# Moving two groups of transposes ahead of the attention products in a fused conditional transformer block

## The reference, cut to what matters

```python
out = (input - mean) * jax.lax.rsqrt(var + EPS) * weight + bias     # layer norm, then + tanh(cond @ lin_w.T + lin_b)
_rmsnorm = lambda x: x * jax.lax.rsqrt(jnp.mean(x * x, axis=-1, keepdims=True) + EPS)
attn = jax.nn.softmax(scale * jnp.einsum('bnqd,bnkd->bnqk', q, k), axis=-1)
o = jnp.einsum('bnqk,bnkd->bnqd', attn, v)                           # then @ W_o.T
ffn = jax.nn.silu(x @ gate_w.T) * (x @ hidden_w.T) @ out_w.T + out_b
x = x + a_alpha * attention(gamma * _rmsnorm(x) + beta)
return x + f_alpha * ffn(gamma2 * _rmsnorm(x) + beta2)
```

## Time and profile before

| | us |
|---|---|
| median of 3 executions (995.45 to 999.46) | 995.79 |
| profiled execution, its own time | 997.22 |
| span of the profiled execution | 995.4 |
| TensorE matmul busy | 944.1 (95%) |
| TensorE weight loads busy | 906.4 (91%) |
| VectorE, ScalarE, GpSimd busy | 715.6, 615.2, 584.6 |

### The profile page before, as it was taken

The page is one execution under the profiler, slowest core; times in us unless marked ns, Lnnn a source line. Parts: engine busy times, 40 slices in busy tenths (PEclk is TensorE's granted clock), DMA queues, the critical chain, the costliest instruction groups (busy, mean ns, idle before and its releaser), DMA issues.

```text
span 995.4 us, 28347 instructions
## 1 busy us (share of the span) xinstructions
PE 944.1 (95%) x11164; PEld 906.4 (91%) x11164; DVE 715.6 (72%) x1355; ACT 615.2 (62%) x1733; POOL 584.6 (59%) x531
## 2 busy tenths in 40 slices
PE   5557899999999999999999999999999999999998
PEld 4446799999999999999999999999999999999997
DVE  6654687777777778777777777777777876766654
ACT  4343676667666766676667666766776676666432
POOL 4445765756667675757576575666757475544320
PEclk9776799999999999999999999999999999999999
DMA  7000001000010000001000100100010000000000
GB/s 234 22 23 1 23 2 33 13 12 33 13 33 4 31 13 18 27 13 34 13 23 13 34 13 12 34 12 33 2 33 13 12 13 13 13 12 12 12 12 22
DMA packets 20930, 23.33 MB, mean 23 GB/s; under 512 B 1216, under 2 KB 20288, under 8 KB 20800
## 3 DMA queue, kind: packets, MB, share of 16 engines
q1 hardware_dynamic: 20800, 21.54, 6.6%
HBM read 13.15 MB, written 8.39 MB: 22 GB/s over the span
## 4 chain that ended last, share of the span: by engine, by line
PE 92%; DVE 4%; issue 2%; POOL 1%; ACT 1%; DMA 0%; SPq 0%; DVEq 0%; ACTq 0%; POOLq 0%
PE psum L293 18%; PE psum L295 18%; PE psum L294 18%; PE psum L432 6%; PE psum L507 6%; PE psum L506 6%; PE psum L505 6%; PE psum L408 4%; PE psum L448 4%; PE psum L323 2%; PE psum L342 2%; DVE least L632 1%; PE psum L331 1%; PE psum L501 1%; PE psum L335 1%
## 5 line engine op out<-in xcount | busy, mean ns | idle before, releaser
L293 PE MATMUL psum<-xf_hi,ffn_hi 128*128 128x256 f32 x1024 | 289.6, 283 | 2.1 <-ACT probsT L908 1.6
L295 PE MATMUL psum<-xf_hi,ffn_lo 128*128 128x256 f32 x1024 | 286.0, 279 | 0.0
L294 PE MATMUL psum<-xf_lo,ffn_hi 128*128 128x256 f32 x1024 | 285.9, 279 | 0.0
L900 ACT ACTIVATE probs<-psum,least 128x64 f32<-128x64 f32 x928 | 204.6, 354 | 55.6 <-DVE least L632 55.0
L1096 POOL TENSOR_TENSOR probs<-probs,inv_sum 128x512 f32<-128x512 f32 x128 | 133.4, 1044 | 126.9 <-DVE inv_sum L653 126.2
L293 PEld LDWEIGHTS psum<-xf_hi,ffn_hi 128*128 128x128 f32 x1024 | 192.2, 188 | 3.2 <-issue 2.8
L295 PEld LDWEIGHTS psum<-xf_hi,ffn_lo 128*128 128x128 f32 x1024 | 192.4, 188 | 0.0
L294 PEld LDWEIGHTS psum<-xf_lo,ffn_hi 128*128 128x128 f32 x1024 | 192.0, 187 | 0.0
L929 ACT ACTIVATE prod_hi<-late 128x512 fp32r<-128x512 f32 x128 | 83.5, 653 | 114.3 <-DVE late L711 114.2
L507 PE MATMUL psum<-prod_hi,ffn_lo 128*128 128x256 f32 x512 | 143.2, 280 | 0.0
L506 PE MATMUL psum<-prod_lo,ffn_hi 128*128 128x256 f32 x512 | 143.0, 279 | 0.0
(11 more groups left out here) (106 smaller groups left out, 2244.6 us busy)
## 6 DMA issues: line engine op xcount, KB each, us to landing
out_t_dram<-x_res SPq DMA_DIRECT2D x31, 256.0 KB, 2.2
xin<-x_dram SPq DMA_DIRECT2D x15, 512.0 KB, 4.0
w_raw<-attn_w_dram SPq DMA_DIRECT2D x1, 1024.0 KB, 7.5
x_res<-gate_w_dram SPq DMA_DIRECT2D x1, 1024.0 KB, 10.2
late<-hidden_w_dram SPq DMA_DIRECT2D x1, 1024.0 KB, 11.7
w_raw<-out_w_dram SPq DMA_DIRECT2D x1, 1024.0 KB, 6.4
xin<-x_dram SPq DMA_DIRECT2D x2, 256.0 KB, 2.9
k_heads<-mod_w_dram SPq DMA_DIRECT2D x1, 320.0 KB, 4.4
```

Of the source, the lines that this page charges most:

```text
L293: pe.matmul(out, stat_hi, mov_hi, start=first, stop=False)
L294: pe.matmul(out, stat_hi, mov_lo, start=False, stop=False)
L295: return pe.matmul(out, stat_lo, mov_hi, start=False, stop=last)
L900: op = act.activation(probs[g % 2][:, h * SEQ:(h + 1) * SEQ], scores[g % 2][:, h // 2, h % 2], ACT.Exp, bias=least[g % 2][:, h:h + 1], sca ...
```

## The change

The two groups of norm transposes, with the waits for their bank, become a function `norm_item`. From slot 12 on it is called directly behind `turn_probs`, ahead of `score_banks_free`, `times_values` and `score`. Up to slot 11 it stays behind the scores. No instruction is added or taken away, and the other engines' lists are as they were.

```diff
+            def norm_item(s):
+                grp, j = s // PSEQ, s % PSEQ
+                norm_bank_free(s)
+                if j == 0 and is_part(grp + 2):
+                    turn_x(grp + 2)
+                if j == 2 and is_group(grp) and s >= 0:
+                    spread_inverses(grp)
+
@@
                     for g in (s - 2, s - 1):
                         if is_seq(g):
                             turn_probs(g)
+                    if s >= FFN_AT:
+                        norm_item(s)
                     score_banks_free(s)
@@
-                if s % 2 == 0 or s < 0:
-                    norm_bank_free(s)
-                if j == 0 and is_part(grp + 2):
-                    turn_x(grp + 2)
-                if j == 2 and is_group(grp) and s >= 0:
-                    spread_inverses(grp)
+                if (s % 2 == 0 or s < 0) and s < FFN_AT:
+                    norm_item(s)
```

## The result

The changed kernel has a median of 1004.93 us (1003.18 to 1005.39, 6 executions) against 998.08 for the kernel before, measured beside it (6 executions, one of them disturbed; 996.70 without that one); the ratio is 1.0067 with a 95% interval of 1.0052 to 1.0082, so slower by 6.7 us. 1000.0 us, a ratio of 1.0042, had been forecast with a range up to 1002.8. The disturbed execution, of 1838.4 us, is left out of the ratio.

A forecast was written before the change was run, and what follows sets the result against it. TensorE, busy without a gap from 140 to 900 us, was taken to bound the kernel. Full slots' +3.7 us and odd slots' +0.5 made +4.2 on 995.79, so 1000.0 us, with a range of 995.6 to 1002.8.

The forecast's parts named there:

- What bounds the kernel, and what the move does to TensorE's packing: TensorE has no gap from 140 to 900 us; four transposes cost 0.44 us in the new place, 0.37 in the old.
- Rival A: The gap behind the scores goes, the projection following at its usual step: -0.14 us a slot, 989 us; chance 0.08.
- rival B: Transposes cost 0.09 us each in the new place too, so full slots give 0: 996 us; chance 0.15.
- Its bounds: Transpose step in the new place: 0.09 us gives nothing, 0.12 gives 5.8 us; range stated as 999.0 to 1000.9 us.
- Its size: Full slots from first turned probability to first gate matmul: +0.07 us each, 53 of them, +3.7 us.
- The odd slots: Slots 12, 122, 126 and 130: +0.1, +0.07 at worst, +0.22 and +0.10 us, nothing in 134; together +0.5 us.
- The moved waits: Norm transposes ask 1.2 us earlier for bank, x or inverse RMS and still find them; margin 1.3 us.
- The scores come later: Scores 0.44 us later; ahead of hidden in inverse-RMS slots some 0.07 us of slack is left, wait costed at nothing.
- Rival C: New wait ahead of hidden in 27 inverse-RMS slots; 0.1 us beyond the slack adds 2.7 us, 1002.7 us; chance 0.22.
- The base: Median of the kernel before, 995.79 us, to which the forecast added 4.2 us.
- What would show it: Timeline signs: 4.16 us from first turned probability to gate, keys 0.67 us behind scores' start, no TensorE wait 140 to 900 us.

The follow-up runs named there:

- x_only: Changed kernel with only the transposes of x moved, those of the inverse RMS left behind the scores; 1.0016 of the kernel before.
- keep_even_inv: Changed kernel, but the inverse-RMS transposes of the even groups stay behind the scores; 1.0012 of the kernel before.
- before_late: Kernel before plus a 0.42 us VectorE instruction behind both least-score searches in even groups' inverse-RMS slots, spare tile placed behind `stats`; 1.0109 of the kernel before.
- late_even: Kernel before plus a 0.42 us VectorE instruction behind both least-score searches in even groups' inverse-RMS slots, spare tile behind all others; 1.0004 of the kernel before.

## Where the prediction was right and where it was wrong

- **What bounds the kernel, and what the move does to TensorE's packing**: right. The twelve transposes stand at steps of 0.11 us: 8 take 0.88 (510.35 - 509.47) and the four of x 0.53 with the gap behind them. The gap behind the scores moved ahead of the projection, as slot 120 had shown. Rival A, a gain, is refuted, and rival B, no change, too: a slot costs more.
- **Its bounds**: the prediction's own bounds of the step, 0.09 and 0.12 us, give 996.3 and 1002.1 us, not the 999.0 to 1000.9 that it gives its 0.55 for, and rival B stands at 996 in one place and at 995.6 in another.
- **Its size**: 0.05 instead of 0.07 us a slot. The term that was off is the distance from scores to keys, 0.62 us and not slot 120's 0.67; against that the first keys matmul holds the second back by 0.23 instead of 0.20. 2.7 us in place of 3.7 (2.5 unrounded). By the rule on tile shapes of TensorEngine Tiling (Array Packing) in the Trainium skill, Key Properties, the move would be free, since there are as many changes of shape as before; the trace has the gaps at these changes, alike in both kernels (0.20, 0.15 and 0.20 us from start to start, with 0.11 between transposes), but 0.05 us more a slot.
- **The odd slots**: in slot 126 +0.23 us came (0.22 forecast), in slot 130 +0.05 (0.10, with bounds 0 and 0.2). At the end of the stretch behind slot 124 nothing of it is left (85.33 and 85.34 us), which the prediction did not foresee: from 66 to 73 us behind slot 124, just behind a wait of both kernels, 60 matmuls of 256 columns stand 0.113 us apart in the changed kernel and 0.118 in the one before. Why they do is open. In slot 12 the transposes themselves cost the 0.1 us forecast, and the waits behind them, 0.8 us, had been left out.
- **The moved waits**: right. TensorE finds bank, x and inverse RMS ready; nothing is held up ahead of the transposes from 125 to 900 us.
- **The scores come later**: this is the step that failed. I followed the 0.44 us as far as hidden of the same slot, found 0.07 us of cover left, and costed the wait at nothing. That cover did hold: there is no wait ahead of hidden in the inverse-RMS slots. But "slots with the inverse RMS are where that counts" was wrong. VectorE is not the only one who waits for the scores: by way of the least scores ScalarE's exponentials do, and ScalarE, and VectorE behind it, hand the delay on without idle time of their own to take it up. It was still whole, 0.43 us, 14 us later in the next slot with x, where in odd groups the merge leaves no room and the squares' load stood 0.07 us behind its release. Price: 12 times 0.38 us, which is 4.6 us; with the like in slot 17 and in the group of slot 12 it is 5.6 us.
- **Rival C** had the mechanism, a wait of TensorE ahead of hidden from later scores, and the right sign, but the wrong slot, and 27 places where there were 12; the larger of the two waits, ahead of the squares, it did not have. Its condition ("from 0.07 us on") was that of a place where nothing happened. What spoke against it, that TensorE had no gap from 140 to 900 us before, was no argument: a list without waits doesn't tell how near they are. That the range's upper edge, 1002.8, was set from this rival, and lies near what the ratio makes of 995.79 (1002.5), is luck.
- **The base**: 1004.93 us is 4.9 us above the forecast, but the change is only 2.5 us dearer than forecast by the ratio (6.7 for 4.2). The rest is the 995.79 on which the forecast stood, a median of three; beside the experiments the kernel before has medians of 997.23 to 997.53, from 14 to 29 executions.
- **"What would show it"** served: 4.14 us a slot (4.16 forecast), but a wait of TensorE between 140 and 900 us where none should have been.
- **Open**: what makes the gap behind the scores; why gate and hidden behind the squares are 0.1 us shorter in some groups of x_only and keep_even_inv; and why some stretches of matmuls stand at 0.113 us.

## What to carry to other kernels

When an edit makes a result later, follow the delay through every engine that waits for it until a row with enough idle time ahead of it is reached, and not just to the next wait of the bounding engine; here two engines, one waiting for the other, handed on a delay of 0.4 us undiminished over 14 us, while a delay put on one of them alone was gone at the next wait. Where slots alternate, look for the slot of the period that has extra work, for there the cover is thinnest, and compute it as the distance from release to waiter, because neither a list of waits nor a busy time of 100% shows any of it. And a gap that stands ahead of a group of instructions may belong to the group ahead of it: a slot in which the group is missing tells.

## What the runs showed of the hardware

- The 24 bytes a partition of before_late's new tile, placed ahead of most others, made TensorE's matmuls of 256 columns stand 0.120 us apart instead of 0.118 in the whole kernel, at a granted clock of 1.00: gate and hidden took 2.88 instead of 2.83 us, and in the same 400 us TensorE did 4839 matmuls where it had done 4877. With the same tile behind all others (late_even) it did 4875. The kernel was 1.1% slower, and the list of waits has no new wait of TensorE to put it down to. Both rows are of the busy time from 500 to 900 us, before_late first:

```profile
500.00:900.00 400.00, 400.00 (x4839) 387.53 (x4839) 297.35 (x556) 266.91 (x782) 247.59 (x222) 1.00 0.06 18
```

```profile
500.00:900.00 400.00, 400.00 (x4875) 387.13 (x4875) 301.66 (x558) 268.84 (x789) 249.24 (x223) 1.00 0.06 18
```

The two kernels differ in nothing but the tile's place, and so in the places of those behind it; which of them matters, and why, was not taken further.

- The first 104 to 108 us, in which the granted clock changes several times, differ by up to 4 us between profiled executions of code that is the same to there, about the size of the effect that was sought. Start to start within the steady stretch of the kernel before, slots of one kind repeat within 0.02 us.
